# A graph network's first layer taken in steps of two groups of edges instead of one

## What is computed

```python
h = x @ W1 + b1
e = concatenate([h[dst], h[src] - h[dst]], axis=-1)
m = relu(relu(e @ W2 + b2) @ W3 + b3)
x = layernorm(x + relu(segment_max(m, dst)))
AX = segment_sum(edge_weight[:, None] * x[src], dst)
x = layernorm(x + AX @ WL.T + bL)
```

## Time and profile before

| what | value |
|---|---|
| median of 3 runs | 2501.72 us |
| lowest and highest | 2500.84 and 2503.64 us |
| the profiled execution | 2503.72 us |
| its span (first to last instruction) | 2501.9 us |
| mean granted TensorE clock | 0.922 |
| busy: PE, DVE, ACT, POOL | 78%, 64%, 32%, 51% of the span |
| first layer's loop | about 150 to 1366 us |

### The profile page before, as it was taken

The page is one execution under the profiler, slowest core; times in us unless marked ns, Lnnn a source line. Parts: engine busy times, 40 slices in busy tenths (PEclk is TensorE's granted clock), DMA queues, the critical chain, the costliest instruction groups (busy, mean ns, idle before and its releaser), DMA issues.

```text
span 2501.9 us, 60027 instructions
## 1 busy us (share of the span) xinstructions
PE 1942.2 (78%) x15568; PEld 1699.8 (68%) x15568; DVE 1609.3 (64%) x4451; ACT 807.9 (32%) x2385; POOL 1278.0 (51%) x1300
## 2 busy tenths in 40 slices
PE   4757678777777778777776359899999997888884
PEld 4646556555565556556554259889888897888884
DVE  3547667767676766767677745445444453888887
ACT  0423233333333333333333125555555554000003
POOL 6246566666666666666663706666666666000000
PEclk7769899999999999998998569999999999999997
DMA  4245455555555555555554227777777776888885
GB/s 120 80 114 154 135 153 151 152 151 151 153 147 151 152 152 149 152 151 152 150 153 109 56 80 237 241 242 242 240 240 244 243 240 220 263 266 267 264 266 169
DMA packets 528061, 447.25 MB, mean 179 GB/s; under 512 B 58459, under 2 KB 493111, under 8 KB 527968
## 3 DMA queue, kind: packets, MB, share of 16 engines
q1 hardware_dynamic: 336516, 208.08, 29.6%
q0 software_dynamic: 53312, 138.17, 17.8%
q10 hardware_dynamic: 138140, 100.06, 13.3%
HBM read 300.43 MB, written 145.64 MB: 178 GB/s over the span
## 4 chain that ended last, share of the span: by engine, by line
PE 47%; issue 14%; another core or an unknown queue 13%; DVE 12%; ACT 4%; DVEq 2%; SPq 2%; DMA 2%; POOL 2%; ACTq 1%; POOLq 0%
PE z_ps L1489 6%; PE t_ps L1489 6%; PE m_ps L1489 6%; PE m_ps L1513 4%; PE z_ps L1415 4%; DVE run L1013 4%; PE z_ps L1513 3%; PE m_ps L1402 3%; PE t_ps L1424 2%; PE t_ps L1513 2%; PE m_ps L1403 2%; DVE whole L991 2%; POOL whole L433 1%; DVEq L1211 1%
## 5 line engine op out<-in xcount | busy, mean ns | idle before, releaser
L426 POOL DMA_INDIRECT whole<-q_tab,src_ti x784 | 763.0, 973 | 485.4 <-remote 237.9
L445 POOL DMA_INDIRECT tab<-whole,row_at x392 | 406.1, 1036 | 281.3 <-issue 83.2
L1143 DVE TENSOR_SCALAR whole<-row_bc,node_id 128x768 f32<-128x768 uint8 x392 | 229.7, 627 | 317.2 <-DMA row_bc<-rel_tab 257.7
L1402 PE MATMUL m_ps<-ident,whole 128*128 128x128 f32 x1568 | 333.7, 292 | 57.3 <-issue 45.0
L654 ACT ACTIVATE m<-m_ps,bias 128x512 f32<-128x512 f32 x196 | 134.7, 687 | 669.7 <-remote 623.0
L1403 PE MATMUL m_ps<-oh,win 128*128 128x128 f32 x1568 | 318.6, 286 | 6.4 <-issue 6.4
L1402 PEld LDWEIGHTS m_ps<-ident,whole 128*128 128x128 f32 x1568 | 262.9, 207 | 79.0 <-issue 76.0
L1200 DVE TENSOR_TENSOR whole<-whole 128x384 f32<-128x384 f32 x440 | 241.6, 550 | 58.9 <-issue 37.9
L1403 PEld LDWEIGHTS m_ps<-oh,win 128*128 128x128 f32 x1568 | 254.0, 203 | 15.6 <-issue 15.5
L940 DVE TENSOR_TENSOR scratch<-s_ps,blk_oh 128x196 f32<-128x196 f32 x196 | 70.6, 360 | 299.6 <-remote 279.3
L1013 DVE TENSOR_TENSOR_SCAN run<-row_bc,run,z_ps 128x512 f32<-128x512 uint8 x195 | 248.2, 1273 | 0.4 <-ACT z_ps L659 0.2
(11 more groups left out here) (281 smaller groups left out, 3509.2 us busy)
## 6 DMA issues: line engine op xcount, KB each, us to landing
win<-p_tab SPq DMA_DIRECT2D x784, 64.0 KB
seg_tab<-run_e ACTq DMA_DIRECT2D x196, 256.0 KB
win<-xw_tab SPq DMA_DIRECT2D x392, 128.0 KB
whole<-tab SPq DMA_DIRECT2D x220, 200.0 KB
whole<-tab ACTq DMA_DIRECT2D x220, 200.0 KB
row_bc<-seg_row_tab SPq DMA_DIRECT2D x196, 128.0 KB
row_bc<-rel_tab SPq DMA_DIRECT2D x196, 96.0 KB
whole<-q_tab,src_ti POOLq DMA_INDIRECT x784
```

The costliest lines, as they stand in the source:

```text
L426: pool.indirect_dma_start(qg[:, g % RING, j, :], None, q_tab[:, :], IOA(ap=src_ti[:, t:t + 1], axis=0)).then_inc(q_ld[g % RING], 16)
L445: pool.indirect_dma_start(tab[:, :], IOA(ap=row_at[0:FR, k:k + 1], axis=0), fat[0:FR, k % RR, :], None).then_inc(fat_st[k // GK % RS], 16)
L1143: last = V.tensor_scalar(pick[:, s, j, :], row_bc[:, s, 0:GK * SLOTS], node_id[:, j:j + 1], None, ALU.is_equal)
L1402: mm(m1_ps[:, s, c], lhsT=qg[:, r % RING, j, :], rhs=ident[:], start=True, stop=False)
```

## The change

The first layer is taken in steps of two groups (a pair). GpSimd waits once for a pair and then issues its eight gathers, two pairs in front (`LEAD = 2`). VectorE handles both groups of a pair by one instruction where it can (one-hots, counts, slots, rows), adds the first rows itself (two additions a pair instead of PE's `firsts_added`), and copies the counts (`tensor_copy` into `many`) that ScalarE copied. The four parts of `values_split` stand in front of the loop instead of in its first four steps. ScalarE alternates `relu_2` of one pair with `relu_1` of the next. SyncE loads windows for two groups after one wait, and one row table for two groups. PE's signals `slot_ps`, `vals_ps` come once a pair. The tables `edge_oh` and `edge_row` lie where the node tables were, so the loads of rows start after `p_tab` is stored. `values` now comes two pairs behind, and the batch of four groups (`SB`) is gone.

```diff
+LEAD = 2
-SB = 4
-ST = SB * GT
+ST = 2 * GT
...
-            for g in range(G):
-                if g >= AHEAD:
-                    pool.wait_ge(m1_done, g - AHEAD + 1)
-                for j in range(GT):
-                    t = GT * g + j
-                    pool.indirect_dma_start(qg[:, g % RING, j, :], None, q_tab[:, :], IOA(ap=src_ti[:, t:t + 1], axis=0)).then_inc(q_ld[g % RING], 16)
+            for u in range(G // 2):
+                if u >= LEAD:
+                    pool.wait_ge(m1_done, 2 * (u - LEAD) + 2)
+                for g in (2 * u, 2 * u + 1):
+                    for j in range(GT):
+                        t = GT * g + j
+                        pool.indirect_dma_start(qg[:, g % RING, j, :], None, q_tab[:, :], IOA(ap=src_ti[:, t:t + 1], axis=0)).then_inc(q_ld[g % RING], 16)
...
+            for v in range(G // 2 + 2):
+                if 2 * v + UN < G:
+                    sp.wait_ge(m1_done, 2 * v + 2)
                     sp.sem_inc(sp_waited, 1)
-                    windows(p_tab, g + UN)
-                if LATE <= g and g - LATE + RB < G:
-                    sp.wait_ge(run_done, g - LATE + 1)
+                    for g in (2 * v + UN, 2 * v + UN + 1):
+                        windows(p_tab, g)
+                if v >= 2 and 2 * (v - 2) + RB < G:
+                    sp.wait_ge(run_done, 2 * (v - 2) + 2)
                     sp.sem_inc(sp_waited, 1)
-                    rows0(g - LATE + RB)
+                    rows0(v - 2 + RB // 2)
...
-            def step0(i, r):
-                for part, lag in ((relu_1, 2), (relu_2, 3), (run_copy, 4), (many_copy, 2), (store, 4)):
-                    if runs(i, r - lag):
-                        part(i, r - lag)
+            def step0(i, w):
+                for h in range(2):
+                    for part, lag in ((relu_2, 2), (relu_1, 1)):
+                        if runs(i, 2 * (w - lag)):
+                            part(i, 2 * (w - lag) + h)
+                for h in range(2):
+                    if runs(i, 2 * (w - 3)):
+                        run_copy(i, 2 * (w - 3) + h)
+                        store(i, 2 * (w - 3) + h)
...
+            def slots_of(i, w):
+                step = SLOT_STEPS * pair(i, w)
+                a = 2 * w % 4
+                V.tensor_scalar(third[:, :, :], s_ps[:, :, COUNT:COUNT + GK * NBK], THIRD, ROUND, ALU.mult, ALU.add).then_inc(slot_step, 1)
                 dve.wait_ge(slot_step, step + 1)
+                V.tensor_scalar(rows3[:, :, 1:], third[:, :, :].rearrange("p s (c b) -> p (s c) b", b=NBK), ROUND, float(SL), ALU.subtract, ALU.mult
                                 ).then_inc(slot_step, 1)
                 dve.wait_ge(slot_step, step + 2)
+                V.tensor_tensor_scan(first[:, :, :].rearrange("p c b -> p (c b)"), keep[:, :, :].rearrange("p c b -> p (c b)"),
+                                     rows3[:, :, :].rearrange("p c b -> p (c b)"), 0.0, ALU.mult, ALU.add).then_inc(slot_step, 1)
+                dve.wait_ge(slot_step, step + 3)
+                for s in range(2):
+                    last = V.tensor_tensor(picked[:, GT * s:GT * (s + 1), :].rearrange("p (c t) b -> p c t b", t=CK),
+                                           s_ps[:, s, 0:GT * NBK].rearrange("p (c t b) -> p c t b", t=CK, b=NBK),
+                                           first[:, GK * s:GK * (s + 1), 0:NBK].unsqueeze(2).to_broadcast([P, GK, CK, NBK]), ALU.add)
+                last.then_inc(slot_step, 1)
+                dve.wait_ge(slot_step, step + 4)
+                V.tensor_tensor(picked[:, :, :], picked[:, :, :], blk_oh[:, a:a + 2, :, :].rearrange("p s t b -> p (s t) b"), ALU.mult).then_inc(slot_step, 1)
+                V.tensor_copy(many[:, ds(2 * GK * pair(i, w), 2 * GK)].rearrange("p (s c) -> p s c", s=2), s_ps[0:NBK, :, MANY:MANY + GK])
+                dve.wait_ge(slot_step, step + 5)
+                V.tensor_reduce(slot_t[:, ds(2 * GT * pair(i, w), 2 * GT)], picked[:, :, :], axis=AX_X, op=ALU.add).then_inc(slot_done, 1)
...
+            def step0(i, w):
+                if runs(i, 2 * (w - 1), RING):
+                    dve.wait_ge(slot_ps, pair(i, w - 1) + 1)
+                if runs(i, 2 * (w - 3), RING):
+                    values_sum(i, w - 3)
+                if runs(i, 2 * (w - 2), RING):
+                    for h in range(2):
+                        scan(i, 2 * (w - 2) + h)
+                if runs(i, 2 * (w - 1), RING):
+                    slots_of(i, w - 1)
+                if runs(i, 2 * (w + 1), RING):
+                    one_hot(i, w + 1)
+                    block_hot(i, w + 1)
+                if runs(i, 2 * (w - 1), RING):
+                    slots_placed(i, w - 1)
...
-            def step0(i, r):
-                for part, lag in ((gathered, 2), (firsts_added, 2), (values, PERM_LAG + 1), (slots, 1), (second, 3), (by_edge, 4)):
-                    if runs(i, r - lag, RING):
-                        part(i, r - lag)
...
+            def step0(i, w):
+                for part, lag in ((gathered, 0), (second, 1), (by_edge, 2)):
+                    if runs(i, 2 * (w - lag), RING):
+                        for h in range(2):
+                            part(i, 2 * (w - lag) + h)
+                if runs(i, 2 * (w - 2), RING):
+                    values(i, w - 2)
+                if runs(i, 2 * w, RING):
+                    slots(i, w)
```

More of the change, by code:

```diff
@@ L22 @@
 RING = 3 * UN
-RB = 6
-AHEAD = 4
+RB = 3 * UN
+LEAD = 2
 LATE = 2
@@ L343, in i_of, with pair @@
             return n // UN * i + r // UN
+        def pair(i, w, n=RING):
+            return n // 2 * i + w
         def runs(i, r, n=UN):
@@ L1385, in firsts_added @@
-            def firsts_added(i, r):
-                s = r % 2
-                pe.wait_ge(first_done, grp(i, r, RING) + 1)
-                occ = s_ps[:, s, 0:GT * NBK].rearrange("p (c t b) -> p c t b", t=CK, b=NBK)
-                mm(occ, lhsT=three_b[:], rhs=first_b[:, s, :, 0:NBK].unsqueeze(2).to_broadcast([P, GK, CK, NBK]), start=False, stop=True).then_inc(occ_ps, 1)
+                if old(i, 2 * (w - 1), RING):
+                    pe.wait_ge(vals_in, pair(i, w - 1) + 1)
+                pe.wait_ge(perm_ready, pair(i, w) + 1)
@@ new lines, in values @@
+                for s in range(2):
+                    of_chunk = vals_bank[:, s, :].rearrange("p (c v) -> p c v", c=GK)
+                    for c in range(GK):
+                        for j in range(CK):
+                            t = GT * s + CK * c + j
+                            last = mm(of_chunk[:, c, :], lhsT=row_hot[:, w % 2, t, :], rhs=slot_hot[:, w % 2, t, :, :].rearrange("p q v -> p (q v)"),
+                                      start=j == 0, stop=j == CK - 1)
+                last.then_inc(vals_ps, 1)
@@ new lines, in slots @@
+            def slots(i, w):
+                pe.wait_ge(blk_done, pair(i, w) + 1)
+                if old(i, 2 * (w - 1), RING):
+                    pe.wait_ge(slot_done, pair(i, w - 1) + 1)
+                for s in range(2):
+                    hot = blk_oh[:, 2 * w % 4 + s, :, :]
+                    by_chunk = hot.rearrange("p (c t) b -> p t c b", t=CK)
+                    flat = hot.rearrange("p t b -> p (t b)")
+                    occ = s_ps[:, s, 0:GT * NBK]
+                    count = s_ps[:, s, COUNT:COUNT + GK * NBK].rearrange("p (c b) -> p c b", b=NBK)
+                    mm(count, lhsT=ones_b[:], rhs=by_chunk[:, 0], start=True, stop=False)
+                    mm(count, lhsT=ones_b[:], rhs=by_chunk[:, 1], start=False, stop=False)
+                    mm(count, lhsT=ones_b[:], rhs=unit_b[:, :].rearrange("p (c b) -> p c b", b=NBK), start=False, stop=True)
+                    for c in range(GK):
+                        for j in range(CK):
+                            mm(s_ps[0:NBK, s, MANY + c:MANY + c + 1], lhsT=hot[:, CK * c + j, :], rhs=ones_b[:, 0:1], start=j == 0, stop=j == CK - 1)
+                    mm(occ, lhsT=after_b[:], rhs=flat, start=True, stop=False)
+                    last = mm(occ.rearrange("p (c t b) -> p t c b", t=CK, b=NBK)[:, 1], lhsT=ones_b[:], rhs=by_chunk[:, 0], start=False, stop=True)
+                last.then_inc(slot_ps, 1)
```

283 lines of the change are left out of this document (98 added, 185 removed).

## The result

The changed kernel takes 2647.6 us (2629.1 to 2667.6, four runs) beside 2502.7 us of the kernel before on the same chip: a ratio of 1.058 (1.052 to 1.065). It is slower by 145 us; 91 were forecast. Its own runs lie 1.5% apart, those of the kernel before 0.2%. The profiled execution is the fastest of the four: its span is 2627.4 us, 125.5 more than before.

What follows compares the result with a forecast made beforehand. It took PE's signals, held behind GpSimd's back-to-back DMA issues, as the bound. 11.67 + 1.5 = 13.17 us a pair, +0.94 over 94.5 pairs, +2: 2501.7 + 91 = 2593 us; own range 2530 to 2650, 8 in 10 2435 to 2710.

Steps and rivals of the forecast that it cites:

- What bounds the kernel: First layer: PE's signals wait until about 1 us behind GpSimd's back-to-back DMA issues, a loop of 6.07 us a group.
- The series of eight costs more than it saves: First layer's loop: 13.17 us a pair against 12.23 before, +0.94, over 94.5 pairs +89 us.
- GpSimd's 9.86 us: First layer: GpSimd's eight issues after one wait take 9.86 us a pair from first start to last end.
- 0.04 us an issue, the same before and after: Shared access in the first layer: VectorE's instructions lengthen GpSimd's issues by 0.04 us each, unchanged by the edit.
- rival (d): VectorE's product with both inputs in SBUF shuts GpSimd out, 0.56 us a series: +53 on the forecast, 2646 us; chance 0.04.
- PE's stand, 1.5 us a pair: First layer: PE stands after 37 of 72 passes in GpSimd's series; 1.5 us a pair stay uncovered, ends 0 and 3.7.
- rival (a): First layer: PE never stands; 11.14 to 11.67 us a pair, -51 to -101, about 2425 us; chance 0.29.
- Rival (b): slot_ps misses the opening between series, VectorE starts late; one in three steps gives 14.5 us a pair, 2715 us; chance 0.14.
- the slot signal misses the opening: slot_ps, PE's last signal of a step, is held; VectorE's 6.3 and PE's 2.0 us then lie open; chance 0.14.
- VectorE's pair, 9.2 to 10 us, hidden: First layer: VectorE's work on a pair takes 9.2 us, with waits up to 10, under 11.67, so it costs nothing.
- Start and end, +2: Ends of the first layer: -3 us at the start, +5 us at the end, together +2.
- VectorE idle for over 4 us (b): Sign against the forecast: VectorE idle for more than 4 us before its first scan, pointing to the late slot signal.

Runs made afterwards that it cites:

- b_series8: Kernel before with only GpSimd's wait changed: one wait before every second group, so eight gathers issue in a series; 2695.8 us, 1.0755 of the kernel before.
- a_series4: Changed kernel plus a GpSimd wait for slot_ps in the middle of each series, so four gathers issue in a series; 2502.6 us, 1.0006 of the kernel before.
- a_narrow: Changed kernel with each gather behind the first 12 groups fetching 16 bytes of a row; 2699.7 us, 1.068 of the kernel before.
- a_relu_order: Changed kernel with ScalarE making both relu_1 of a pair before both relu_2 of the pair before; 2687.9 us, 1.063 of the kernel before.

## Why the prediction was right or wrong

- *What bounds the kernel:* right, on the chips that hold signals. Without GpSimd's gathers the delay of 4.2 us is 0.03 us, and the kernel before takes 13% less. It isn't a bound of the kernel everywhere: on two other chips four runs of the changed kernel's variants don't show it.
- *The series of eight costs more than it saves:* right, and shown both ways (`b_series8` +7.6%, `a_series4` no change). With the series broken, the rest of the change moves the time by less than 0.2% on such a chip.
- *GpSimd's 9.86 us and "0.04 us an issue, the same before and after":* wrong. 1.040 against 0.968 us makes 0.6 us a pair. The instruction that does most of it is not the product with both inputs in SBUF, which I had weighed as rival (d), but the one-hot L971, which I had costed at nothing: with it cut to an eighth the mean is 0.968 again. The row of L991 that I took as evidence against was misread, since that issue had begun before L991 did.
- *PE's stand, 1.5 us a pair:* the step that was weakest. It made every pair alike. The stand is there as forecast, passes 0.7 to 1.4 us apart, and so is what follows from it: in 53 pairs PE has 17 passes left behind the series. But it doesn't come from a count of passes: the series that starts at 1019.1 has 89 passes in it, and no two of them start more than 0.6 us apart. The 41 pairs of 11.87 us lie near what rival (a) gave (11.14 to 11.67), the others up to 17.9 us. That their mean, 13.44, lies so near to the forecast's 13.17 is in part luck: GpSimd's series took 10.45 us in place of 9.86, and the time from its end to the next series 2.99 in place of 3.31 (1.57 + 0.24 + 1.5), so the second error took away half of the first.
- *Rival (b), "the slot signal misses the opening":* the event is there, in 53 of 94 pairs and not in one in three, and these pairs take 2.8 us more than the others, not 8.3. VectorE's waits are 5.4 us each (151.0 / 28). That VectorE's lateness is what costs wasn't shown: `b_series8` loses more with steps that don't wait for `slot_ps` first, and the run with the scans ahead of the wait fell on chips without the hold.
- *The granted clock:* no term had it. It fell from 0.94 to 0.83 in the loop: PE stands, and runs at half of its clock for some us afterwards (812 to 816: 0.65). It is part of the 14.66 and wasn't separated.
- *VectorE's pair, 9.2 to 10 us, hidden:* right (9.27 without gathers; `a_series4` pays none of it).
- *Start and end, +2:* the start gives 0.8 us (forecast 3): the 25th gather starts at 182.48 in place of 183.27. The first gather starts 7 us earlier, but the first four now take 1.79, 3.80, 2.42 and 2.85 us, beside the conversions moved in front of the loop, and the second signal comes at 180.0, later than the 177.02 of before. The end costs 13.1 (forecast 5).

Sign and range held; the median lies 2.4 us inside the upper end of the forecast's own range (2650), and two of the four runs lie outside. Two signs that I had named as wrong showed as well: VectorE idle for over 4 us (b), and issues over 1.0 us on average (d). The median is 54.6 us over the forecast: 25 of them are the loop's (94 x 0.27), 18.5 the distance of the profiled execution to the median of four runs that lie 1.5% apart, and the other 11 the end and the start (8 and 2). The cause of the spread wasn't shown. Open are also: by what path GpSimd's issues hold PE's signals, whether the issue or its packets do it, why some chips do it and others don't, and, on a chip that does, whether a gap twice as long or scans ahead of the wait would give the loss back. No version that does the whole work beat the kernel before.

## What to carry to other kernels

Where GpSimd issues many indirect DMAs, look for the time between a matmul's end and the first instruction that waits for it, and, where signals are held, keep the series short: a wait for `slot_ps` in the middle of a series of eight was worth all of the loss. A mean period that fits a forecast proves little; look at the single periods before believing the mechanism, since steps of 11 and of 17 us can average to your number. When one row speaks against a lock between two engines, look which instruction began first. And compare only on one chip: the same kernel took 2217 and 2531 us here, and close variants of one change cost 6% on one chip and 2% on two others.

## What the runs showed of the hardware that was not expected

- PE's signals, held for 4.2, 5.8 and 6.5 us (rows above) under series of four and eight of GpSimd's DMA issues on some chips, and on others not at all under a series of 784.
- The hold doesn't depend on the bytes that the DMAs move (16 or 512 a row: 1.068 for `a_narrow` and 1.063 for `a_relu_order`, on one chip).
- An indirect DMA issue that begins while VectorE compares two SBUF operands with bf16 output ends about 0.82 us behind that comparison: 1.84 us with 1024 elements (1.22 us), 1.38 with 512 (0.69 us), in place of 0.94. An issue that began 0.40 us before the comparison took 0.98. VectorE's scans (1.27 us, reading PSUM) lengthen none: of 133 issues of the kernel before that lie beside such a scan alone, the longest took 0.96.
- Work of one engine that blocks a second can go with signals of a third getting out: cutting it cost 5%.
